# Cross-attention: softmax sums from a column of ones in the value tiles, output turned and normalised token by token

## Chip, cores and metric

The kernel runs on one NeuronCore of one Trainium2 chip, in one launch. The metric is device time in microseconds (us), from the start of the program to its end. Before the change it is 1276.02 us, the median of 3 runs (1275.25 to 1277.25).

## What is computed

One decoder layer over `x` of shape (16, 128, 256): a sparse self-attention, a cross-attention to a context of the same shape, and a mixture-of-experts feed-forward, each with a layer norm ahead of it and a residual behind it. Only the cross-attention bears on the change. Cut to what matters:

```python
x = x + self_attention(layernorm(x), ...)
x = x + xattn(layernorm(x), ctx, ctx)
x = x + experts(layernorm(x), ...)

def xattn(q, k, v):          # each (16, 128, 256); 8 heads
    qh = q.reshape(16 * 8, 16, 256)       # a head is 16 of the 128 rows
    kh = k.reshape(16 * 8, 16, 256)
    vh = v.reshape(16 * 8, 16, 256)
    qk = einsum('bdm,bdn->bmn', qh, kh) / sqrt(16)
    return einsum('bmn,bcn->bcm', softmax(qk, -1), vh).reshape(16, 128, 256)
```

So a head attends along the feature axis: 256 query columns m against 256 key columns n, and the 16 rows of the head are the contraction of the scores and the channels of the value.

## The kernel before, in words

Each engine runs its own program; they meet at semaphores only. The cross-attention stage is written by `cross_loads` (SP, the DMA queue), `cross_tensor` (PE), `cross_scalar` (ACT), `cross_vector` (DVE) and `cross_pool` (POOL). All five walk the same steps i = -4 to 17 (`STEPS`), as a software pipeline written out by hand, each step cut in four parts k = 0 to 3. In step i the stage works on several batches at once:

- `max_scores(i + 2)` on PE (line 1278): 8 times two matmuls of 112x256 into one of two banks (`XMAX`). `reduce_max` on DVE (line 1393) takes the row maxima of each bank; the next use of a bank waits for it.
- `shift_transposes(i + 1)` on PE (1289) turns the 8 maxima of a token, after all 8 reductions of that batch; ACT negates them (`keep_shift`, 1348) and SP writes them as a row of the query tile by DMA (1232).
- `score(i, k)` on PE (1264): two matmuls of 114x512 that give scores minus maxima into two of four banks; `softmax` on ACT (1341) writes the exponentials, 128x512 each, to `probs4`. `ctx_transposes` (1296) and `keep_values` (1356, 1357) make the value tile `xvalue`.
- `values(i - 1, piece)` on PE (1311), in pieces 0 to 7 of 4 matmuls, each 32 output rows wide, on fp32 data: pieces 0 to 3 multiply the probabilities by `xvalue` and pieces 4 to 7 by `ones_x`, so that the bank `XPV` holds the sums in its left half and each denominator, repeated for 16 rows, in its right half. In the trace each such matmul is two instructions, so a batch has 64. Pieces 0 to 2 follow in part k = 1, 3 to 5 in k = 2, 6 and 7 in k = 3.
- `normalised(i - 2)` on DVE: a reciprocal of 128x256 (1401), a multiplication (1403) into `xout`; it comes between reductions 0 and 1 of step i. `residual(i - 2)` on POOL (1448) adds `xout` to `X`, `next_stats` on DVE (210) takes the statistics for the next layer norm.
- `query_(i + 4)` on DVE (251) normalises the next queries, `query_high` on ACT (1364) makes their rounded part and `query_low` on POOL (1443) the rest; SP writes both to memory (1237, 1239) and reads them back head by head (1219), with the keys (1212), each queue entry in a fixed order.

PE executes in program order, so that whatever a matmul waits for holds up all that stands behind it. The order on PE in a step before is

```python
for k in range(4):
    score(i, k)
    if k == 0: shift_transposes(i + 1)
    if k == 2: ctx_transposes(i)
    max_scores(i + 2, 2 * k); max_scores(i + 2, 2 * k + 1)
    for piece in ((), (0, 1, 2), (3, 4, 5), (6, 7))[k]: values(i - 1, piece)
```

After the last batch the next stage (`moe_vector`, line 1725) waits until `X` is complete.

Of the kernel before, what the change touches and what calls it, by code (L numbers as in the profile page):

```python
# [7 lines left out]
ALU = mybir.AluOpType  # L8
ACT = mybir.ActivationFunctionType
# [3 lines left out]
B, T, D = 16, 128, 256  # L13
# [15 lines left out]
XH, XC = 8, 16  # L29
# [35 lines left out]
def build(nc, io):  # L65
    ctx = ExitStack()
    with ctx:
        place = [ctx]

        def sb(name, shape, dt=F32):  # L70
            return place[0].enter_context(nc.sbuf_tensor(name, shape, dt))
# [1107 lines left out]
        xvalue = [sb(f"xvalue{p}", [128, 2, XH, 32]) for p in range(2)]  # L1179
        ones_x = sb("ones_x", [128, 2, 32])  # L1180
        xmax = [sb(f"xmax{p}", [128, 2, XH]) for p in range(2)]
        xshift = [sb(f"xshift{p}", [XH, D], F32R) for p in range(2)]
        xden = sb("xden", [128, D])
        xout = [sb(f"xout{p}", [128, D]) for p in range(2)]
# [20 lines left out]
        def cross_loads(sp):  # L1205
# [19 lines left out]
            for b in range(B + 3):  # L1225
# [19 lines left out]
                if b < B:  # L1245
                    if b >= 2:
                        sp.wait_ge(S(f"ld_heads{p}"), 128 * (b // 2))
                    if b >= 4:
                        sp.wait_ge(S("xscore_done"), 4 * (b - 3))
                    load_keys(b, p, s)  # L1250
                    sp.wait_ge(S(f"xq_out{p}"), 32 * (b // 2 + 1))
                    load_queries(b, p, s)


        def cross_tensor(pe):
            def score(b, k):

                s = b % 4
                if k == 0:
                    pe.wait_ge(S(f"ld_shift{b % 2}"), 32 * (b // 2 + 1))  # L1260
                if 4 * b + k >= 2:
                    pe.wait_ge(S("xprob_ready"), 2 * (4 * b + k - 1))
                for c in range(2):
                    last = nc.tensor.matmul(XSCORE[2 * (k % 2) + c][:].rearrange("p (t m) -> p t m", t=2),  # L1264
                                            keys_x[s][0:XROWS + 2, k, c * 128:c * 128 + 128],
                                            query_x[s][0:XROWS + 2, k, :, :], start=True, stop=True)
                last.then_inc(S("xscore_done"), 1)

# [30 lines left out]

            def values(b, piece):  # L1300

                if piece == 0:
                    pe.wait_ge(S("xvalue_ready"), b + 1)
                    pe.wait_ge(S("xprob_ready"), 8 * b + 8)
                    if b:
                        pe.wait_ge(S("xpv_read"), b)
                den, hh, c = piece // 4, piece // 2 % 2, piece % 2
                for j in range(4):
                    h = 2 * j + hh
                    lhsT = ones_x[:, hh, :] if den else xvalue[b % 2][:, c, h, :]  # L1310
                    last = nc.tensor.matmul(XPV[32 * j:32 * j + 32, den * D:den * D + D], lhsT,  # L1311
                                            probs4[b % 2][:, 2 * (h % 4) + c, h // 4 * D:h // 4 * D + D],
                                            start=piece % 4 == 0, stop=piece % 4 == 3)
                if piece == 7:
                    last.then_inc(S("xpv_done"), 1)

            pe.wait_ge(S("cross_zeroed"), 2)
            pe.wait_ge(S("attn_added"), B)
            for i in STEPS:
                for k in range(4):  # L1320
                    if 0 <= i < B:
                        score(i, k)
                    if k == 0 and 0 <= i + 1 < B:
                        shift_transposes(i + 1)
                    if k == 2 and 0 <= i < B:
                        ctx_transposes(i)
                    if 0 <= i + 2 < B:
                        max_scores(i + 2, 2 * k)
                        max_scores(i + 2, 2 * k + 1)
                    if 0 <= i - 1 < B:  # L1330
                        for piece in ((), (0, 1, 2), (3, 4, 5), (6, 7))[k]:
                            values(i - 1, piece)


        def cross_scalar(act):
            def softmax(b, k):
                act.wait_ge(S("xscore_done"), 4 * b + k + 1)
                if k == 0 and b >= 2:
                    act.wait_ge(S("xpv_done"), b - 1)
                for c in range(2):  # L1340
                    nc.scalar.activation(probs4[b % 2][:, 2 * k + c, :], XSCORE[2 * (k % 2) + c][:], ACT.Exp,  # L1341
                                         scale=XSCALE).then_inc(S("xprob_ready"), 1)

# [6 lines left out]
            def keep_values(b):  # L1350
                act.wait_ge(S("ctxT_done"), b + 1)
                if b >= 2:
                    act.wait_ge(S("xpv_done"), b - 1)
                out = xvalue[b % 2][:].rearrange("p c (j two) x -> p (c j) (two x)", two=2)
                src = XT[:, 0:D].rearrange("p (j two x) -> p j two x", two=2, x=XC)
                nc.scalar.copy(out[:, :, 0:XC], src[:, :, 0, :])
                nc.scalar.copy(out[:, :, 48:64], src[:, :, 1, :]).then_inc(S("xvalue_ready"), 1)

# [11 lines left out]
            for i in STEPS:  # L1370
                for k in range(4):
                    if 0 <= i < B:
                        softmax(i, k)
                    if k == 0 and 0 <= i + 1 < B:
                        keep_shift(i + 1)
                    if k == 2 and 0 <= i < B:
                        keep_values(i)
                    if k == 1 and 0 <= i + 4 < B:
                        query_high(i + 4)


        def cross_vector(dve):
            def query_(b):
                if b >= 2:
                    dve.wait_ge(S("xq_lo_ready"), b - 1)
                normalise(xq[b % 2][:], b).then_inc(S("xq_ready"), 1)

            def reduce_max(b, m):
# [8 lines left out]
            def normalised(b):  # L1397
                dve.wait_ge(S("xpv_done"), b + 1)
                if b >= 2:
                    dve.wait_ge(S("xdone"), b - 1)  # L1400
# [9 lines left out]
            for p in range(2):  # L1410
                last = nc.vector.memset(xvalue[p][:], 0.0)
            nc.vector.memset(ones_x[:], 0.0).then_inc(S("vector_steps"), 1)
            dve.wait_ge(S("vector_steps"), 7)
            nc.vector.memset(ones_x[:, 0, 0:XC], 1.0)
            nc.vector.memset(ones_x[:, 1, XC:2 * XC], 1.0)
            for s in range(4):
# [5 lines left out]
            for i in STEPS:  # L1422
                for k in range(4):
                    if 0 <= i + 2 < B:
                        reduce_max(i + 2, 2 * k)
                    if k == 0 and 0 <= i - 2 < B:
                        normalised(i - 2)
                    if 0 <= i + 2 < B:
                        reduce_max(i + 2, 2 * k + 1)
                    if k == 1 and 0 <= i + 4 < B:  # L1430
                        query_(i + 4)
                    if k == 2 and 0 <= i - 2 < B:
                        next_stats(i - 2)


        def cross_pool(pool):
            def query_low(b):
                p = b % 2
# [6 lines left out]

            def residual(b):
                pool.wait_ge(S("xpv_read"), b + 1)
                nc.gpsimd.tensor_tensor(X[:, b, :], X[:, b, :], xout[b % 2][:], ALU.add).then_inc(S("xdone"), 1)
# [275 lines left out]
        def moe_vector(dve):  # L1724
            dve.wait_ge(S("xdone"), B)
            nc.vector.memset(zero_b[:], 0.0)
            nc.vector.memset(zero_b4[:], 0.0)
            nc.vector.memset(combine[:], 0.0).then_inc(S("moe_zeroed"), 1)
            ln_stats_vector(dve, 4)
# [303 lines left out]
```

## Time and profile before

| | |
|---|---|
| median of 3 runs | 1276.02 us |
| the profiled execution's own time | 1277.34 us |
| its span, first to last instruction | 1275.6 us |
| mean granted TensorE clock | 0.933 of full speed |
| busy: PE / DVE / ACT / POOL | 89% / 49% / 43% / 48% |
| self-attention and before | up to about 430 us |
| cross-attention | about 430 to 656 us |
| routing and experts | about 656 us to the end |

Busy shares are averages over stages with different limits. The rows further down are from the stage that is changed: a row of a window says how long each engine was busy in a stretch and what clock TensorE was granted (1.00 is 2.4 GHz, 0.50 is 1.2 GHz); a row of a timeline gives start, duration, engine, line, operation, tiles and count, and in brackets how long the engine stood idle before and what ended that.

### The profile page before, as it was taken

How to read it: one execution, taken by the hardware profiler on the slowest of the kernel's cores; microseconds unless marked ns; L12 is line 12 of the kernel's file. 1: busy time of each engine (PE TensorE's matmuls, PEld its weight loads, DVE VectorE, ACT ScalarE, POOL GpSimd, SP SyncE). 2: the span in 40 equal slices, each digit the busy share in tenths (PEclk: the TensorE clock that was granted, in tenths of full speed). 3: DMA queues.
4: the chain of work that ended last, by engine and by line, in shares of the span. 5: the costliest groups of instructions: out<-in, count | busy, mean ns of one | idle time of the engine just before them, and what ended most of it. 6: DMA issues, size and time to landing. Idle time of an engine off the chain costs nothing.

```text
span 1275.6 us, 23609 instructions
## 1 busy us (share of the span) xinstructions
PE 1137.3 (89%) x7920; PEld 911.9 (71%) x7920; DVE 628.4 (49%) x1343; ACT 553.9 (43%) x1185; POOL 612.5 (48%) x755
## 2 busy tenths in 40 slices
PE   5979999999999387878856899999999999999997
PEld 4757777777776254545444788888888788888886
DVE  5656777777777366566556233233233332323323
ACT  3326666666666334444443333333333233333331
POOL 3766565656563201110000566666666566666663
PEclk8969999999999668899885899999999999999998
DMA  5201010101010174344000544443344444334441
GB/s 121 59 1 30 25 31 22 28 25 31 23 29 23 35 164 97 90 103 100 19 1 22 128 108 115 115 110 102 105 114 116 119 115 115 104 104 109 115 115 54
DMA packets 74965, 96.99 MB, mean 76 GB/s; under 512 B 20412, under 2 KB 55868, under 8 KB 74892
## 3 DMA queue, kind: packets, MB, share of 16 engines
q1 hardware_dynamic: 74892, 96.05, 29.1%
q8 instruction: 42, 0.69, 0.2%
q14 instruction: 31, 0.25, 0.1%
HBM read 82.73 MB, written 13.12 MB: 75 GB/s over the span
## 4 chain that ended last, share of the span: by engine, by line
PE 56%; DVE 6%; issue 2%; ACT 1%; DMA 1%; POOL 0%; SPq 0%; POOLq 0%; DVEq 0%; ACTq 0%
PE bank L1589 28%; PE bank L1601 15%; PE bank L1311 5%; PE bank L1264 3%; PE bank L1278 2%; DVE xden L1401 2%; DVE xmax L1393 1%; DVE xout L1403 1%; DMA comb<-combine_scratch 0%; PE bank L1296 0%; PE bank L1289 0%; DVE X L1801 0%; DVE keys_x L1417 0%; PE bank L1564 0%; PE bank L1574 0%
## 5 line engine op out<-in xcount | busy, mean ns | idle before, releaser
L1815 POOL TENSOR_TENSOR hidden<-act_u,comb 128x512 f32<-128x512 f32 x132 | 217.5, 1648 | 214.9 <-DVE act_u L1783 144.0
L1783 DVE TENSOR_TENSOR act_u<-act_g,bank 128x512 f32<-128x512 f32 x132 | 90.8, 688 | 393.8 <-PE bank L1589 365.2
L1689 ACT ACTIVATE act_g<-bank 128x512 f32<-128x512 f32 x132 | 78.9, 598 | 356.5 <-PE bank L1589 356.5
L1589 PE MATMUL bank<-x_hi,up_hi 128*128 128x512 f32 x528 | 209.0, 396 | 5.8 <-POOL up_lo L1820 5.8
L1589 PE MATMUL bank<-x_lo,up_hi 128*128 128x512 f32 x528 | 208.2, 394 | 0.0
L1589 PE MATMUL bank<-x_hi,up_lo 128*128 128x512 f32 x528 | 206.5, 391 | 0.0
L1601 PE MATMUL bank<-down_hi,h_hi 128*128 128x256 f32 x528 | 149.4, 283 | 1.8 <-POOL down_lo L1825 1.8
L1601 PE MATMUL bank<-down_hi,h_lo 128*128 128x256 f32 x528 | 150.1, 284 | 0.0
L1601 PE MATMUL bank<-down_lo,h_hi 128*128 128x256 f32 x528 | 150.0, 284 | 0.0
L833 ACT ACTIVATE probs<-bank 128x512 f32<-128x512 f32 x192 | 113.8, 604 | 81.3 <-PE bank L656 44.5
L1393 DVE TENSOR_REDUCE xmax<-bank 128x2 f32<-128x512 f32 x128 | 83.5, 686 | 73.3 <-PE bank L1278 73.3
L1589 PEld LDWEIGHTS bank<-x_hi,up_hi 128*128 128x128 f32 x528 | 100.5, 190 | 25.0 <-POOL up_lo L1820 7.2
L1589 PEld LDWEIGHTS bank<-x_hi,up_lo 128*128 128x128 f32 x528 | 99.9, 189 | 21.9
L1341 ACT ACTIVATE probs<-bank 128x512 f32<-128x512 f32 x128 | 68.9, 590 | 107.4 <-PE bank L1264 107.4
L1589 PEld LDWEIGHTS bank<-x_lo,up_hi 128*128 128x128 f32 x528 | 100.5, 190 | 16.0
L1820 POOL TENSOR_TENSOR up_lo<-up_in,up_hi 128x512 fp32r<-128x512 f32 x66 | 85.0, 1287 | 48.1 <-ACT up_hi L1701 48.1
L1601 PEld LDWEIGHTS bank<-down_hi,h_hi 128*128 128x128 f32 x528 | 101.4, 192 | 7.1 <-POOL down_lo L1825 2.0
L1601 PEld LDWEIGHTS bank<-down_lo,h_hi 128*128 128x128 f32 x528 | 101.4, 192 | 5.0
L1601 PEld LDWEIGHTS bank<-down_hi,h_lo 128*128 128x128 f32 x528 | 101.5, 192 | 0.0
L1278 PE MATMUL bank<-keys_x,query_x 112*128 112x256 f32 x256 | 57.8, 346 | 48.0 <-DVE xmax L1393 28.1
L1787 DVE TENSOR_TENSOR h_lo<-hidden,h_hi 128x512 fp32r<-128x512 f32 x132 | 90.5, 686 | 1.8 <-ACT h_hi L1695 1.8
L952 DVE TENSOR_REDUCE blockmax<-bank 128x32 f32<-128x512 f32 x96 | 64.8, 690 | 51.9 <-PE bank L609 51.9
(258 smaller groups left out, 2246.3 us busy)
## 6 DMA issues: line engine op xcount, KB each, us to landing
comb<-combine_scratch SPq DMA_DIRECT2D x132, 256.0 KB, 3.9
up_in<-in_w_up SPq DMA_DIRECT2D x66, 256.0 KB, 3.5
down_in<-in_w_down SPq DMA_DIRECT2D x66, 128.0 KB, 3.8
keys_x<-key_rows_x SPq DMA_DIRECT2D x32, 192.0 KB, 3.3
key_rows_x<-ctx_hi SPq DMA_DIRECT2D x256, 16.0 KB, 1.5
query_x<-xq_rows_hi SPq DMA_DIRECT2D x64, 64.0 KB, 3.1
ctx_in<-in_ctx SPq DMA_DIRECT2D x16, 128.0 KB, 2.0
key_rows_x<-ctx_lo SPq DMA_DIRECT2D x128, 16.0 KB, 1.5
```

Of the source, the lines that this page charges most:

```text
L833: nc.scalar.activation(probs[:, u, :], SCORE[u % 2][:], ACT.Exp, scale=SCALE)\
L952: ins = nc.vector.tensor_reduce(blockmax[:, s, :, c0:c0 + 4], SMAX[m % 2][:].rearrange("p (h c k) -> p h c k", h=KV, k=BLK), AX, ALU.max)
L1278: last = nc.tensor.matmul(XMAX[m % 2][:, n * D:n * D + D], query_x[s][0:XROWS, k, pair // 2, c * 128:c * 128 + 128], keys_x[s][0:XROWS, k, ...
L1341: nc.scalar.activation(probs4[b % 2][:, 2 * k + c, :], XSCORE[2 * (k % 2) + c][:], ACT.Exp, scale=XSCALE).then_inc(S("xprob_ready"), 1)
L1393: nc.vector.tensor_reduce(xmax[b % 2][:, m // 4, hs:hs + 2], XMAX[m % 2][:].rearrange("p (h n) -> p h n", h=2), AX, ALU.max).then_inc(S(f" ...
L1589: last = nc.tensor.matmul(out[:], wp[p][:, c, s, :], xp[:, c, t:t + 512], start=k == 0, stop=k == 5)
L1601: last = nc.tensor.matmul(OUT[k // 2][:, k % 2 * D:k % 2 * D + D], hp[h][:, q * 128:q * 128 + 128], wp[p][:], start=False, stop=True, skip ...
L1689: nc.scalar.activation(act_g[h][:], GATE[h][:], ACT.Silu).then_inc(S(f"gated{h}"), 1)
L1783: nc.vector.tensor_tensor(act_u[h][:], act_g[h][:], UP[h][:], ALU.mult).then_inc(S(f"upped{h}"), 1)
L1787: nc.vector.tensor_tensor(h_lo[h][:], hidden[h][:], h_hi[h][:], ALU.subtract)\
L1815: nc.gpsimd.tensor_tensor(hidden[h][:], act_u[h][:], comb[p][:, 512 * h:512 * h + 512], ALU.mult)\
L1820: nc.gpsimd.tensor_tensor(up_lo[p][:], up_in[p][:], up_hi[p][:], ALU.subtract)\
```

## The change

The value tile gets a column of ones behind the 16 value columns of each head, so one matmul gives sums and denominator; `ones_x` and the four pieces that used it go. Both value groups (`hh` = 0 and 1, even and odd heads) are written to the two halves of the bank in one stretch. ACT copies that bank to `xpv`, PE transposes it in four 128x128 blocks into another bank (`XOUT`), DVE takes reciprocals of 128x16 and multiplies into `xnorm`, PE transposes that back in two blocks, and DVE adds it to `X`. Steps are cut in eight parts u instead of four, each with one score matmul pair half as large as before; the score banks are three instead of four. `query_` moves from DVE to POOL, the residual from POOL to DVE. `normalised` is a step earlier.

```diff
-        XSCORE = [bank[0], bank[1], bank[2], bank[3]]
-        XMAX = [bank[4], bank[5]]
-        XPV, XT = bank[6], bank[7]
+        XSCORE = [bank[0], bank[1], bank[2]]
+        XMAX = [bank[3], bank[4]]
+        XPV, XOUT, XT = bank[5], bank[6], bank[7]
...
+            def score(b, u):
+                s, k, c, n = b % 4, u // 2, u % 2, XH * b + u
...
+                if n >= 3:
+                    pe.wait_ge(S("xprob_ready"), n - 2)
+                nc.tensor.matmul(XSCORE[n % 3][:].rearrange("p (t m) -> p t m", t=2),
...
-            def values(b, piece):
+            def values(b, hh):
+                if hh == 0:
+                    pe.wait_ge(S("xvalue_ready"), b + 1)
+                    pe.wait_ge(S("xprob_ready"), 8 * b + 8)
+                    if b:
+                        pe.wait_ge(S("xpv_kept"), b)
+                for c in range(2):
+                    for j in range(4):
+                        h = 2 * j + hh
+                        last = nc.tensor.matmul(XPV[32 * j:32 * j + 32, hh * D:hh * D + D], xvalue[b % 2][:, c, h, :],
+                                                probs4[b % 2][:, 2 * (h % 4) + c, h // 4 * D:h // 4 * D + D],
+                                                start=c == 0, stop=c == 1)
...
+            def turn_values(b):
+                pe.wait_ge(S("xpv_kept"), b + 1)
+                if b:
+                    pe.wait_ge(S("xdone"), b)
+                for n in range(4):
+                    last = nc.tensor.transpose(XOUT[:, n * 128:n * 128 + 128], xpv[:, n * 128:n * 128 + 128], ident[:])
+                last.then_inc(S("xturned"), 1)
+
+            def turn_back(b):
+                pe.wait_ge(S("xnormed"), 2 * b + 2)
+                for n in range(2):
+                    last = nc.tensor.transpose(XOUT[:, n * 128:n * 128 + 128], xnorm[:, n * 128:n * 128 + 128], ident[:])
+                last.then_inc(S("xturned"), 1)
...
             for i in STEPS:
+                for u in range(XH):
                     if 0 <= i < B:
+                        score(i, u)
+                    if u == 0 and 0 <= i + 1 < B:
                         shift_transposes(i + 1)
+                    if 0 <= i + 2 < B:
+                        max_scores(i + 2, u)
+                    if u == 0 and 0 <= i - 2 < B:
+                        turn_back(i - 2)
+                    if u == 2 and 0 <= i - 1 < B:
+                        values(i - 1, 0)
+                        values(i - 1, 1)
+                    if u == 5 and 0 <= i - 1 < B:
+                        turn_values(i - 1)
+                    if u == 3 and 0 <= i < B:
                         ctx_transposes(i)
...
         def cross_scalar(act):
...
+                nc.scalar.copy(xvalue[b % 2][:, :, :, 0:XC], XT[:, 0:D].rearrange("p (c h x) -> p c h x", c=2, x=XC))\
+                    .then_inc(S("xvalue_ready"), 1)
+            def keep_pv(b):
+                act.wait_ge(S("xpv_done"), b + 1)
+                if b:
+                    act.wait_ge(S("xturned"), 2 * b - 1)
+                nc.scalar.copy(xpv[:], XPV[:]).then_inc(S("xpv_kept"), 1)
...
+                for u in range(XH):
                     if 0 <= i < B:
+                        softmax(i, u)
+                    if u == 0 and 0 <= i + 1 < B:
                         keep_shift(i + 1)
+                    if u == 2 and 0 <= i + 4 < B:
+                        query_high(i + 4)
+                    if u == 4 and 0 <= i - 1 < B:
+                        keep_pv(i - 1)
+                    if u == 5 and 0 <= i < B:
                         keep_values(i)
...
         def cross_vector(dve):
...
             def normalised(b):
-                nc.vector.reciprocal(xden[:], XPV[:, D:2 * D]).then_inc(S("xden_ready"), 1)
-                dve.wait_ge(S("xden_ready"), b + 1)
-                nc.vector.tensor_tensor(xout[b % 2][:], XPV[:, 0:D], xden[:], ALU.mult).then_inc(S("xpv_read"), 1)
+                dve.wait_ge(S("xturned"), 2 * b + 1)
+                src = XOUT[:].rearrange("p (hh mj x) -> p hh mj x", hh=2, x=32)
+                nc.vector.reciprocal(xden[:], src[:, :, :, XC]).then_inc(S("xnormed"), 1)
+                dve.wait_ge(S("xnormed"), 2 * b + 1)
+                nc.vector.tensor_tensor(xnorm[:]..., src[:, :, :, 0:XC], xden[:]..., ALU.mult).then_inc(S("xnormed"), 1)
+            def residual(b):
+                dve.wait_ge(S("xturned"), 2 * b + 2)
+                nc.vector.tensor_tensor(X[:, b, :], X[:, b, :], XOUT[:, 0:D], ALU.add).then_inc(S("xdone"), 1)
...
+                for u in range(XH):
                     if 0 <= i + 2 < B:
+                        reduce_max(i + 2, u)
+                    if u == 1 and 0 <= i - 2 < B:
+                        residual(i - 2)
+                    if u == 3 and 0 <= i - 2 < B:
                         next_stats(i - 2)
+                    if u == 6 and 0 <= i - 1 < B:
+                        normalised(i - 1)
...
         def cross_pool(pool):
+            def query_(b):
+                if b >= 2:
+                    pool.wait_ge(S("xq_lo_ready"), b - 1)
+                x = X[:, b, :]
+                nc.gpsimd.tensor_scalar(xq[b % 2][:], x, mean[:, b:b + 1], rstd[:, b:b + 1], ALU.subtract, ALU.mult)\
+                    .then_inc(S("xq_ready"), 1)
...
-            for i in STEPS:
-                if 0 <= i - 2 < B:
-                    residual(i - 2)
-                if 0 <= i + 4 < B:
-                    query_low(i + 4)
+            pool.wait_ge(S("xbias_ready"), 1)
+            for b in range(B):
+                query_(b)
+                query_low(b)
```

## Rows read from the trace of the kernel before

**Rows 1.** Windows: us; busy (instructions) PE, PEld, DVE, ACT, POOL; clock; DMA share; GB/s
```profile
320.00:420.00 100.00, 93.14 (x787) 71.80 (x785) 70.22 (x183) 64.56 (x136) 47.77 (x90) 1.00 0.10 25
447.84:460.98 13.14, 10.81 (x35) 8.11 (x36) 9.98 (x17) 0.86 (x2) 1.45 (x2) 0.50 0.78 165
468.45:478.23 9.78, 9.24 (x94) 5.45 (x92) 6.21 (x11) 5.50 (x13) 0.73 (x1) 1.00 0.62 149
480.07:493.16 13.09, 10.80 (x93) 6.19 (x92) 7.90 (x13) 5.27 (x14) 1.45 (x2) 0.87 0.39 90
519.24:530.72 11.48, 9.18 (x93) 5.61 (x92) 7.90 (x14) 5.27 (x14) 1.45 (x2) 1.00 0.45 106
618.88:630.18 11.30, 9.01 (x84) 5.38 (x84) 6.95 (x11) 3.71 (x10) 0.72 (x1) 0.85 0.05 14
638.10:646.01 7.91, 6.53 (x74) 3.32 (x74) 2.61 (x3) 4.56 (x11) 0.73 (x1) 1.00 0.00 0
```

**Rows 2.** Timeline of DVE: reciprocals of batch 0 and 11, then one step
```profile
480.07 1.75 DVE L1401 RECIPROCAL xden<-bank 128x256 f32<-128x256 f32 x1
...
618.88 1.75 DVE L1401 RECIPROCAL xden<-bank 128x256 f32<-128x256 f32 x1
...
568.26 1.75 DVE L1401 RECIPROCAL xden<-bank 128x256 f32<-128x256 f32 x1
570.04 0.42 DVE L1403 TENSOR_TENSOR xout<-bank,xden 128x256 f32<-128x256 f32 x1
570.39 1.97 DVE L1393 TENSOR_REDUCE xmax<-bank 128x2 f32<-128x512 f32 x3
```

**Rows 3.** Timeline of PE: one step at full clock
```profile
560.08 1.50 PE L1311 MATMUL bank<-probs,xvalue 128*32 128x256 f32 x24
561.51 0.73 PE L1264 MATMUL bank<-query_x,keys_x 114*128 114x512 f32 x2
562.08 0.38 PE L1296 MATMUL bank<-ident,ctx_v 128*128 128x128 f32 x2
562.21 0.72 PE L1278 MATMUL bank<-keys_x,query_x 112*128 112x256 f32 x4
562.86 0.64 PE L1311 MATMUL bank<-probs,xvalue 128*32 128x256 f32 x8
...
571.12 0.50 PE L1278 MATMUL bank<-keys_x,query_x 112*128 112x256 f32 x2 [2.22 <-DVE xmax L1393]
```

**Rows 4.** Timeline, end of the stage: PE's last values, POOL's residual, DVE's statistics
```profile
648.37 1.93 PE L1311 MATMUL bank<-probs,xvalue 128*32 128x256 f32 x32 [2.43 <-DVE xout L1403]
650.10 1.94 PE L1311 MATMUL bank<-probs,ones_x 128*32 128x256 f32 x32
...
655.14 0.43 DVE L210 BATCH_NORM_STATS2 stats<-X 128x6 f32<-128x256 f32 x1 [0.83 <-POOL X L1448]
```

**Rows 5.** Groups by line and shape: nearest rows for what is new
```profile
L1341 ACT ACTIVATE probs<-bank 128x512 f32<-128x512 f32 x128 | 68.9, 590 | 107.4 <-PE bank L1264 107.4
L840 ACT COPY pv<-bank 128x512 f32<-128x512 f32 x32 | 18.9, 592 | 1.1 <-PE bank L687 1.1
L973 DVE RECIPROCAL weight<-bank 128x32 f32<-128x32 f32 x32 | 11.0, 344 | 5.1 <-PE bank L698 5.1
L399 POOL TENSOR_SCALAR gates<-gates 128x96 f32<-128x96 f32 x16 | 9.8, 617 | 0.0
L251 DVE TENSOR_SCALAR xq<-X,mean,rstd 128x256 f32<-128x256 f32 x16 | 6.4, 406 | 0.0
```

**Rows 6.** Timeline of PE in the self-attention: four transposes and what follows
```profile
421.75 0.66 PE L698 MATMUL bank<-ident,pv 128*128 128x128 f32 x4
422.34 0.64 PE L687 MATMUL bank<-probs,value_near 128*32 128x256 f32 x8
```

**Rows 7.** Timeline of SP, the DMA queue
```profile
553.62 0.80 SPq L1212 DMA_DIRECT2D keys_x<-key_rows_x  x2
...
557.27 1.31 SPq L1232 DMA_DIRECT2D query_x<-xshift  x2
```

More of the change, by code:

```diff
@@ L1179, in build @@
         xvalue = [sb(f"xvalue{p}", [128, 2, XH, 32]) for p in range(2)]
-        ones_x = sb("ones_x", [128, 2, 32])
         xmax = [sb(f"xmax{p}", [128, 2, XH]) for p in range(2)]
         xshift = [sb(f"xshift{p}", [XH, D], F32R) for p in range(2)]
-        xden = sb("xden", [128, D])
-        xout = [sb(f"xout{p}", [128, D]) for p in range(2)]
+        xpv = sb("xpv", [128, 512])
+        xden = sb("xden", [128, 2, XH])
+        xnorm = sb("xnorm", [128, D])
         XROWS = 64 + 3 * XC
-        XSCORE = [bank[0], bank[1], bank[2], bank[3]]
-        XMAX = [bank[4], bank[5]]
-        XPV, XT = bank[6], bank[7]
+        XSCORE = [bank[0], bank[1], bank[2]]
+        XMAX = [bank[3], bank[4]]
+        XPV, XOUT, XT = bank[5], bank[6], bank[7]
         MAX_ORDER = (0, 2, 1, 3)
@@ L1255, in cross_tensor @@
         def cross_tensor(pe):
-            def score(b, k):
-                s = b % 4
-                if k == 0:
+            def score(b, u):
+                s, k, c, n = b % 4, u // 2, u % 2, XH * b + u
+                if u == 0:
                     pe.wait_ge(S(f"ld_shift{b % 2}"), 32 * (b // 2 + 1))
[L1261 to L1267, printed above, removed]
+                if n >= 3:
+                    pe.wait_ge(S("xprob_ready"), n - 2)
+                nc.tensor.matmul(XSCORE[n % 3][:].rearrange("p (t m) -> p t m", t=2),
+                                 keys_x[s][0:XROWS + 2, k, c * 128:c * 128 + 128],
+                                 query_x[s][0:XROWS + 2, k, :, :], start=True, stop=True)\
+                    .then_inc(S("xscore_done"), 1)
             def max_scores(b, m):
@@ L1305, in values @@
                     if b:
[L1306 to L1314, printed above, removed]
-                    last.then_inc(S("xpv_done"), 1)
+                        pe.wait_ge(S("xpv_kept"), b)
[5 more added lines that the diff above has]
+                                                start=c == 0, stop=c == 1)
+                if hh:
+                    last.then_inc(S("xpv_done"), 1)
+            def turn_values(b):
[10 more added lines that the diff above has]
+                last.then_inc(S("xturned"), 1)
             pe.wait_ge(S("cross_zeroed"), 2)
@@ L1319, in cross_tensor, with softmax @@
             for i in STEPS:
-                for k in range(4):
+                for u in range(XH):
                     if 0 <= i < B:
-                        score(i, k)
-                    if k == 0 and 0 <= i + 1 < B:
+                        score(i, u)
+                    if u == 0 and 0 <= i + 1 < B:
                         shift_transposes(i + 1)
-                    if k == 2 and 0 <= i < B:
-                        ctx_transposes(i)
[L1327 to L1332, printed above, removed]
+                    if 0 <= i + 2 < B:
[8 more added lines that the diff above has]
+                    if u == 3 and 0 <= i < B:
+                        ctx_transposes(i)
         def cross_scalar(act):
-            def softmax(b, k):
-                act.wait_ge(S("xscore_done"), 4 * b + k + 1)
-                if k == 0 and b >= 2:
+            def softmax(b, u):
+                n = XH * b + u
+                act.wait_ge(S("xscore_done"), n + 1)
+                if u == 0 and b >= 2:
                     act.wait_ge(S("xpv_done"), b - 1)
-                for c in range(2):
-                    nc.scalar.activation(probs4[b % 2][:, 2 * k + c, :], XSCORE[2 * (k % 2) + c][:], ACT.Exp,
-                                         scale=XSCALE).then_inc(S("xprob_ready"), 1)
+                nc.scalar.activation(probs4[b % 2][:, u, :], XSCORE[n % 3][:], ACT.Exp, scale=XSCALE)\
+                    .then_inc(S("xprob_ready"), 1)
             def keep_shift(b):
@@ L1411, in cross_vector @@
                 last = nc.vector.memset(xvalue[p][:], 0.0)
-            nc.vector.memset(ones_x[:], 0.0).then_inc(S("vector_steps"), 1)
+            last.then_inc(S("vector_steps"), 1)
             dve.wait_ge(S("vector_steps"), 7)
-            nc.vector.memset(ones_x[:, 0, 0:XC], 1.0)
-            nc.vector.memset(ones_x[:, 1, XC:2 * XC], 1.0)
+            for p in range(2):
+                nc.vector.memset(xvalue[p][:, :, :, XC:XC + 1], 1.0)
             for s in range(4):
@@ L1727, in moe_vector @@
             nc.vector.memset(zero_b4[:], 0.0)
-            nc.vector.memset(combine[:], 0.0).then_inc(S("moe_zeroed"), 1)
+            nc.vector.memset(combine[:], 0.0)
             ln_stats_vector(dve, 4)
```

35 lines of the change are left out of this document (4 added, 31 removed).

## The prediction

> **What bounds the kernel now.** I read the windows first: they say which engine fills the changed stage, and at what clock. The step before any reciprocal takes 9.78 us and PE is busy 9.24 of them (window 468.45) [rows 1]; later steps take 11.48 us at full clock and 13.09 at 0.87. PE holds the pace, but not by its work alone. The timeline of DVE gives the steady pace: reciprocals of batch 0 and batch 11 start at 480.07 and 618.88 us [rows 2], 138.81 us for 11 steps, 12.62 each. Then PE's timeline shows the hole: 2.22 us idle before a pair of `max_scores`, ended by a reduction [rows 3]. DVE shows why [rows 2]: behind reduction 0 stand the reciprocal (568.26 to 570.04) and its product, then reduction 1, whose bank PE wants back. And the hole has a second price: steps are of two kinds, 11.48 us at clock 1.00 and 13.0 to 13.1 at 0.87 [rows 1], 1.6 us dearer. Eight of the 11 are dear (3 x 11.48 + 8 x 13.05 = 138.8, which is the measured sum).
>
> **The terms of a new step**, all at full clock. On PE one score matmul takes 0.285 us of the stream (two from 561.51 to 562.08), a pair of `max_scores` as much (562.21 to 562.86 holds two pairs and a small lag), and a result is there some 0.2 us after the stream has moved on [rows 3].
> - Values: 64 instructions become 32. The stretch of 32 takes 650.10 - 648.37 = 1.73 us [rows 4]; cut in pieces it is 0.06 each (24 in 1.43 [rows 3]), 1.92. I take 1.85, against about 3.85 before: 2.0 us saved.
> - `turn_values`: four transposes, 422.34 - 421.75 = 0.59 us [rows 6]; 0.65 with its weights to load. `turn_back`: half of that, 0.3. No row has them in this stage; bounds are 0.13 a pair (562.08 to 562.21 [rows 3]) and twice the 0.59. So PE saves 1.1 us of its work.
> - ACT: one more copy of 128x512, 0.58 (0.592 [rows 5]); one value copy in place of two, nothing; eight exponentials of 0.59 [rows 5] as before, 4.7. With the queries (0.6), shift and value copies (0.8) about 6.7 us a step, hidden as long as a step is longer.
> - DVE: the reciprocal falls from 1.75 us [rows 2] to one of 128x16. Bounds: 0.344 (128x32 [rows 5]) and 0.11 (1.75 over 256 columns, times 16); I take 0.25. Product 0.42 as before, residual 0.42 (new on DVE), `query_` gone (0.41 [rows 5]). Total with eight reductions at 0.65: 5.2 + 0.25 + 0.42 + 0.42 + 0.42 = 6.7 us instead of about 7.9.
> - POOL: residual gone, `query_` comes. Bounds for 128x256: 0.41 (as fast as DVE) and 1.65 (617 ns for 96 columns, scaled) [rows 5]. It runs ahead of need and has the whole step; only the first delays anything: the first low part of the queries, by 0 to 1.2 us, once. I take 0.5. The Trainium skill, "GPSIMD Engine Reference", section 3.1, gives GpSimd some 2.6 cycles an element where VectorE has one for two-input work; by that, as an estimate, GpSimd would need two to three times DVE's time for this operation, which would cost a few tenths of a microsecond once. No run here shows it yet.
> - SP: the entries are the same. Keys to the shift rows are 557.27 - 553.62 = 3.65 us of issue, and the shift rows 1.31 [rows 7]; with three more entries some 6.3 us. Keys are wanted a whole step after their issue ends, so nothing here waits until a step is under about 8 us.
>
> **The walk through a step.** Zero is the end of the last reduction of the batch, for which `shift_transposes` waits. PE: shift pair to 0.25, max 0 to 0.54, `turn_back` to 0.8, score 1 and max 1 to 1.37, score 2 and max 2 to 1.94, values to 3.8, score 3 and max 3 to 4.37, context to 4.6, score 4 and max 4 to 5.2, score 5 and max 5 to 5.75. `turn_values` waits for ACT: score 4 is read from 5.0, exponential to 5.6, copy to 6.2. A wait of 0.5, then to 6.9; behind it stand score 6 and max 6, out at 7.7. DVE was free at 7.0 (reduction 5); reduction 6 to 8.4, reciprocal and product with their hops to 9.15, reduction 7 to 9.8. PE has meanwhile done score 7, max 7 and the next score 0 by 8.4, and stands idle 1.4 us. So what is late next is DVE's tail of two reductions with the normalisation between them, and the step is 9.8 us. Walking the step before in the same way gives its 11.48, since it is read from the same rows. Small hops are easily missed; I take 9.9.
>
> **The sum** against the profiled execution (1277.3 us; span 1275.6; the median of the runs is 1.3 lower).
> - 11 steps: 11 x (12.62 - 9.9) = 29.9, of which 11 x 1.16 = 12.8 is clock that I expect back.
> - The step of window 468.45 (9.78): nothing. The step of window 618.88, 11.30 to 9.9: 1.4.
> - Two steps without reductions, 7.9 each (window 638.10) [rows 1]: PE's stream 5.9 plus a wait of about 0.9 for ACT's copy, 6.8: 2.2 together.
> - End: before, PE came to the last values at 645.94 (648.37 less 2.43 of waiting), just as the last exponentials ended, and the last statistics end at 655.57 [rows 4]: 9.5 us from the exponentials. After: values 1.85 and hops 0.2, copy 0.7, turning 0.9, reciprocal and product 0.8, turning back 0.5, residual 0.5, statistics 0.5: 5.95. Saved 3.5.
> - Start: -0.5.
> Together 36.5. The experts' stage reads `X` later and is untouched. 1277.3 - 36.5 = 1240.8 for the profiled execution; 1240 for the median.
>
> **Rivals.**
> *The clock falls as before* (0.30). PE still has a hole of 1.4 us and a wait of 0.5 in every step. For: holes of 2.2 us brought half clock in 8 steps of 11. Against: the steps near the end have holes of over 1 us with PE busy 6.53 of 7.91 us at clock 1.00, and the self-attention runs 100 us at 1.00 with PE busy 93% [rows 1]. Price: the 12.8 us are not given back and a little more: 1254. The Trainium skill, "TensorE: Matmul & The Clock Gate", section "A second HAM failure mode: psum-queue depth-cycling", describes just such short idles between groups that make the clock swing. The steps of 13.09 us agree with it; those of 7.91 do not.
> *Slower: PE stays at half clock* (0.04). One mechanism: PE paced by DVE never gets back up. For: the window 447.84 shows PE busy 10.81 of 13.14 us at clock 0.50 throughout, paced by reductions. Price: about 7.7 us of stream becomes some 14, with the DVE tail 16 us a step; 13 x (16 - 12.5) = 45 more, 1322. It decides once PE's dense part no longer brings the clock up; after every hole before, it did, so little chance.
> *A longer ring PE, ACT, DVE* (0.08). `turn_values` has everything behind it. If values, copy, turning and normalisation run one after another with every hop longer, or the strided read of the bank costs DVE double, a step is near 11.5: 13 x 1.6 = 21 more, 1261.
> *The change does not do what it says*, PE's values not shrinking because the two groups in one stretch run slower (0.03): 2 us a step come back, partly under the waits: 1266; with the clock too, 1276, no change.
> *Better* (0.05): the hops hide, DVE's own 6.7 and PE's 7.7 us let a step be 9.0: 1228.
>
> **Numbers.** Forecast 0.50 at 1240, its own range 1230 to 1249. The range takes in the fallen clock with some longer steps: 1230 to 1259. Less than 0.2% (2.5 us) is about what a measurement of this kernel can tell from no change. Faster 0.93, same 0.02, slower 0.05.
>
> **What would show it.** Right: steps of 9.5 to 10.3 us; no reciprocal above 0.35 us; PE's longest idles 1.2 to 1.6 us, ended by a reduction before line 1289's transposes; 32 instructions of values a batch; clock 1.00 over the steady steps. The fallen clock would be seen as steps of two lengths again. The forecast is wrong if `turn_values` waits much over 0.5 us, if DVE's new reads of the turned bank are much over 0.42 us, or if PE waits for a DMA.

## The result, and the profile after

The changed kernel takes 1228.42 us (median of 4 runs, 1227.86 to 1228.62) against 1275.85 for the kernel before in the same comparison: a ratio of 0.9628, 95% interval 0.9612 to 0.9644. It is 47.4 us faster. The forecast was 1240 us with a range of 1230 to 1259: right in direction and in mechanism, short by 11.6 us in size. The result lies 1.6 us outside the range.

The windows of the two traces, cut at the same events, say where the time went. The rows below are of the kernel before, then of the kernel after; columns are start:end, us, busy us and instructions of PE, PEld, DVE, ACT and POOL, the granted clock, DMA share, GB/s. The cuts are: the last term of the layer norm, the first `max_scores`, the first score matmul of step 1, of step 2 and of step 14, the end of the last exponentials, the end of the last statistics.

```profile
439.71:447.84 8.13, 0.00 (x0) 0.03 (x1) 0.82 (x3) 1.69 (x3) 1.40 (x2) 0.50 0.58 161
447.84:468.45 20.61, 18.08 (x62) 13.43 (x63) 15.48 (x26) 6.08 (x14) 2.19 (x3) 0.55 0.77 165
478.23:630.04 151.81, 124.27 (x1108) 74.70 (x1104) 94.15 (x143) 62.25 (x142) 15.93 (x22) 0.90 0.36 86
630.04:646.06 16.02, 13.51 (x154) 7.01 (x150) 5.41 (x8) 9.34 (x21) 1.47 (x2) 1.00 0.01 2
646.06:655.57 9.51, 3.66 (x64) 2.39 (x64) 5.17 (x7) 1.29 (x2) 1.46 (x2) 1.00 0.01 2
655.57:1275.60 620.03, 586.09 (x3288) 513.89 (x3288) 204.28 (x403) 220.87 (x460) 345.50 (x264) 0.95 0.38 102
```

```profile
437.08:445.87 8.79, 0.00 (x0) 0.03 (x1) 0.17 (x1) 1.69 (x3) 7.01 (x7) 0.50 0.54 150
445.87:466.30 20.43, 17.57 (x62) 13.60 (x63) 14.78 (x23) 5.92 (x13) 3.87 (x4) 0.56 0.74 170
466.30:474.80 8.50, 7.49 (x66) 5.18 (x65) 5.13 (x9) 5.92 (x13) 1.93 (x2) 1.00 0.64 151
474.80:585.70 110.90, 90.86 (x795) 64.91 (x793) 76.82 (x145) 70.49 (x144) 18.16 (x19) 1.00 0.49 118
585.70:600.99 15.29, 11.43 (x102) 6.25 (x100) 4.73 (x13) 10.81 (x23) 0.00 (x0) 1.00 0.01 2
600.99:606.55 5.56, 3.03 (x38) 1.75 (x38) 2.32 (x7) 1.87 (x3) 0.00 (x0) 1.00 0.00 0
606.55:1226.10 619.55, 584.90 (x3286) 513.68 (x3288) 204.28 (x402) 220.77 (x460) 345.54 (x264) 0.95 0.38 102
```

Twelve full steps fell from 151.81 to 110.90 us: 40.9 of the 49.5 us between the two spans. Step 1, which is the 9.78 us of [rows 1], is 8.50. The end of the stage is 9.51 before and 5.56 after. The last exponentials of two steps without reductions gave only 0.7. The fill is the same and the start 0.7 longer. The remaining 3.1 us lie outside the change: 2.6 before the stage begins (439.71 against 437.08) and 0.5 behind it. The code ahead of the stage is the same in all kernels here, and the same point came at 437.1 to 440.8 us in the traces of this study, so those 2.6 us are, as far as these traces tell, a difference between executions and not a gain of the change.

One full step on DVE, PE and POOL after the change (timelines; start, duration, instruction, count, idle before; `...` marks rows left out):

```profile
521.34 0.25 DVE L1416 RECIPROCAL xden<-bank 128x16 f32<-128x16 f32 x1
521.62 0.42 DVE L1418 TENSOR_TENSOR xnorm<-bank,xden 128x256 f32<-128x256 f32 x1
521.96 0.68 DVE L1409 TENSOR_REDUCE xmax<-bank 128x2 f32<-128x512 f32 x1
...
529.97 0.69 DVE L1409 TENSOR_REDUCE xmax<-bank 128x2 f32<-128x512 f32 x1 [0.54 <-PE bank L1277]
530.58 0.25 DVE L1416 RECIPROCAL xden<-bank 128x16 f32<-128x16 f32 x1
530.86 0.42 DVE L1418 TENSOR_TENSOR xnorm<-bank,xden 128x256 f32<-128x256 f32 x1
531.20 0.68 DVE L1409 TENSOR_REDUCE xmax<-bank 128x2 f32<-128x512 f32 x1
```

```profile
522.75 0.38 PE L1288 MATMUL bank<-ident,xmax 128*8 128x128 f32 x2 [1.34 <-issue]
522.88 0.48 PE L1277 MATMUL bank<-keys_x,query_x 112*128 112x256 f32 x2
523.20 0.38 PE L1326 MATMUL bank<-ident,xnorm 128*128 128x128 f32 x2
...
524.57 1.93 PE L1309 MATMUL bank<-probs,xvalue 128*32 128x256 f32 x32
526.44 0.50 PE L1263 MATMUL bank<-query_x,keys_x 114*128 114x512 f32 x1
...
528.80 0.65 PE L1320 MATMUL bank<-ident,xpv 128*128 128x128 f32 x4 [0.33 <-ACT xpv L1376]
529.21 0.48 PE L1263 MATMUL bank<-query_x,keys_x 114*128 114x512 f32 x1
529.53 0.40 PE L1277 MATMUL bank<-keys_x,query_x 112*128 112x256 f32 x2
...
531.99 0.38 PE L1288 MATMUL bank<-ident,xmax 128*8 128x128 f32 x2 [1.34 <-issue]
```

The reader is to see three things. The reciprocal is 0.25 us where it was 1.75 [rows 2], and every step is 9.24 us (521.34 to 530.58). The hole on PE has moved, from a pair of `max_scores` [rows 3] to the transposes of the maxima (line 1288), and is 1.34 us instead of 2.22. The trace puts this idle down to "issue"; the row before on DVE tells what it is, since reduction 7 ends at 531.88 and the transposes start at 531.99. And one stretch of 32 value instructions takes 1.87 us (524.57 to 526.44), as costed.

### The profile page after: what moved, and what is told of

Read it like the earlier page. It is cut to its first block, busy times and chain, and to the rows that moved or that the text cites. A ratio compares the mean times of both kernels' runs of the same rounds, so it can differ in the third digit from the quotient of the medians.

```text
span 1226.1 us, 22759 instructions
## 1 busy us (share of the span) xinstructions
PE 1092.5 (89%) x7471; PEld 897.6 (73%) x7504; DVE 605.0 (49%) x1342; ACT 564.5 (46%) x1185; POOL 620.4 (51%) x755
## 4 chain that ended last, share of the span: by engine, by line
PE 55%; DVE 4%; issue 4%; ACT 2%; DMA 1%; POOL 0%; SPq 0%; POOLq 0%; DVEq 0%; ACTq 0%
PE bank L1609 29%; PE bank L1621 15%; PE bank L1309 2%; PE bank L1277 2%; PE bank L1263 2%; DVE xmax L1409 1%; PE bank L1320 1%; ACT xpv L1376 1%; PE bank L1288 1%; DMA comb<-combine_scratch 0%; PE bank L1326 0%; DVE X L1821 0%; DVE keys_x L1438 0%; PE bank L1584 0%; PE bank L1295 0%
## 5 line engine op out<-in xcount | busy, mean ns | idle before, releaser
L833 ACT ACTIVATE probs<-bank 128x512 f32<-128x512 f32 x192 | 113.8, 604 | 81.5 <-PE bank L656 44.7
L1840 POOL TENSOR_TENSOR up_lo<-up_in,up_hi 128x512 fp32r<-128x512 f32 x66 | 85.0, 1288 | 90.8 <-ACT up_hi L1721 90.8
L1356 ACT ACTIVATE probs<-bank 128x512 f32<-128x512 f32 x128 | 71.5, 600 | 39.3 <-PE bank L1263 37.8
L654 PE MATMUL bank<-query,keys 128*128 128x256 f32 x256 | 84.9, 356 | 0.5 <-ACT probs L833 0.4
```

What stands on the lines that cost most here:

```text
L654: nc.tensor.matmul(o, keys[p][:, kvh * 4 + j, :], query[p][:, kvh, 256:512], start=True, stop=False)
L833: nc.scalar.activation(probs[:, u, :], SCORE[u % 2][:], ACT.Exp, scale=SCALE)\
L1356: nc.scalar.activation(probs4[b % 2][:, u, :], XSCORE[n % 3][:], ACT.Exp, scale=XSCALE)\
L1840: nc.gpsimd.tensor_tensor(up_lo[p][:], up_in[p][:], up_hi[p][:], ALU.subtract)\
```

## The experiments

All medians are set against the kernel before in the same comparison; its medians there were 1275.4 to 1276.7 us. The diffs are cut to the lines that matter, with `...` for what is left out.

**1. The kernel before with a narrow reciprocal.** The product repeats 16 denominators, so the output is normalised with other values.

```diff
-                nc.vector.reciprocal(xden[:], XPV[:, D:2 * D]).then_inc(S("xden_ready"), 1)
+                nc.vector.reciprocal(xden[:, 0:16], XPV[:, D:D + 16]).then_inc(S("xden_ready"), 1)
...
```

> The kernel before, with its reciprocal over 16 of the 256 denominators only (the multiplication then repeats those 16, so the cross-attention's output is normalised with other values); nothing else is changed, PE still has its 64 value instructions a batch. Theory (the gain is mostly the hole that the wide reciprocal makes behind reduction 0, and the clock that the hole costs): a full step falls from 12.65 us on average to about 9.8, which is PE's own stream, at clock 1.00; with some 4 us at the end of the stage, about 1238 us. Rival (the gain is mostly PE's halved value work): the hole was only a symptom, a step stays above 11 us, about 1257 us or more.

Measured: 1238.71 us, ratio 0.9704 (0.9687 to 0.9720). The window over 11 steps, and PE's remaining hole:

```profile
479.10:588.88 109.78, 101.06 (x1013) 61.70 (x1012) 70.07 (x133) 57.49 (x133) 15.31 (x21) 1.00 0.50 114
```

```profile
520.38 0.50 PE L1278 MATMUL bank<-keys_x,query_x 112*128 112x256 f32 x2 [0.71 <-DVE xmax L1393]
```

9.98 us a step, at clock 1.00, with all 64 value instructions. So 38 of the 47 us are to be had by the width of the reciprocal alone: 1.5 us a step is the hole (2.22 to 0.71), and the remaining 1.14 are the clock, which is at 1.00 in all of these steps. The rival falls.

**2. The kernel after with its value matmuls issued twice.**

```diff
-                for c in range(2):
+                for c in (0, 1, 0, 1):
                     for j in range(4):
                         h = 2 * j + hh
```

> The kernel after, with each value matmul issued twice in its stretch (same results, 64 instructions a batch again). Theory (PE's stream up to the seventh pair of max_scores, and then DVE's tail, set the step, so that work in the stretch is on the path): each step is 1.87 us longer, 9.24 to 11.1, and the 16 batches add 30 us: about 1258 us. Rival (PE has slack in its idle times of 1.34 and 0.33 us a step): 0.2 to 0.5 us a step, about 1233 us.

Measured: 1258.01 us, ratio 0.9860 (0.9842 to 0.9879). Reciprocals come every 10.96 us, 1.72 more than in the kernel after, where 1.87 were expected; the stretch itself is 1.73 longer (3.66 against 1.93). Work in the stretch of values is on the path to the full; PE's two idle times do not absorb it, since they come later in the step and are as long as before:

```profile
523.42 0.38 PE L1288 MATMUL bank<-ident,xmax 128*8 128x128 f32 x2 [1.34 <-issue]
...
525.25 3.66 PE L1309 MATMUL bank<-probs,xvalue 128*32 128x256 f32 x64
```

**3. The kernel after with the normalisation behind the last reduction.**

```diff
-                    if u == 6 and 0 <= i - 1 < B:
+                    if u == 7 and 0 <= i - 1 < B:
                         normalised(i - 1)
```

> The kernel after, with the normalisation (reciprocal and product) on DVE behind reduction 7 of the step instead of behind reduction 6. Theory (PE waits at shift_transposes for DVE's tail: reduction 6, normalisation, reduction 7): 0.62 us leave the tail, PE's idle of 1.34 becomes 0.72, turn_back then waits some 0.1 to 0.2 us for the product; a step is 8.7 to 8.8 us, about 1222 us. Rival (the tail is not what ends last, or turn_back gives all of it back): 9.24 us a step, 1228 us.

Measured: 1221.37 us, ratio 0.9570 (0.9554 to 0.9586); a step is 8.67 us, and the hole is what it should be:

```profile
519.52 0.38 PE L1288 MATMUL bank<-ident,xmax 128*8 128x128 f32 x2 [0.72 <-DVE xmax L1409]
519.65 0.48 PE L1277 MATMUL bank<-keys_x,query_x 112*128 112x256 f32 x2
520.10 0.44 PE L1326 MATMUL bank<-ident,xnorm 128*128 128x128 f32 x2
```

0.62 us leave the hole, and the step gains 0.57 of them. `turn_back` now starts 0.45 us after the `max_scores` ahead of it (519.65 to 520.10) where it was 0.32. DVE's tail is what a step of the change ends with. This one line beats the change by 7 us.

**4. The kernel after with a reciprocal of 128x256 more**, its result unused.

```diff
...
+                nc.vector.reciprocal(xwide[:], XOUT[:, 0:D])
                 nc.vector.reciprocal(xden[:], src[:, :, :, XC]).then_inc(S("xnormed"), 1)
```

> The kernel after, with one more reciprocal of 128x256 on DVE (1.75 us, its result unused) ahead of the small one, so in the tail for which PE waits. Theory: a step is 1.75 us longer, PE's idle grows from 1.34 to 3.1 us, and with holes above those of the kernel before (2.2 us) the clock falls again in most steps, 1.6 us each time: 12.0 us on average, about 1265 us and clock below 1.00 in the steady steps. Rival (the clock does not hang on the hole but on the density of the rest): steps of 11.0 us at clock 1.00, about 1252 us.

Measured: 1286.70 us, ratio 1.0083 (1.0066 to 1.0101): the changed kernel with a reciprocal as wide as before is slower than the kernel before. The hole, and windows from one small reciprocal to the next:

```profile
519.29 0.59 PE L1289 MATMUL bank<-ident,xmax 128*8 128x128 f32 x2 [2.95 <-issue]
```

```profile
490.75:504.32 13.57, 10.29 (x66) 6.97 (x66) 8.01 (x14) 6.08 (x12) 1.93 (x2) 0.75 0.35 90
...
531.58:543.60 12.02, 8.73 (x66) 6.53 (x66) 8.02 (x14) 6.08 (x12) 1.94 (x2) 0.86 0.47 101
```

At full clock a step would be 10.9 us, an estimate from 9.24 and the longer hole. The steps are 12.0 to 13.6, 13.1 on average over twelve (475.58 to 632.76); the clock is 0.75 in eight of the twelve and 0.86 in four. So a longer hole, with the same stream on PE, brings the clock down. I had priced this at 1.1 us a step and it is 2.2.

**5. The same with half that width** (128x128), which makes the hole as long as in the kernel before.

```diff
...
+                nc.vector.reciprocal(xwide[:], XOUT[:, 0:128])
```

> The kernel after, with one more reciprocal of 128x128 on DVE (some 0.87 us, unused) ahead of the small one: PE's idle becomes about 2.2 us, as long as in the kernel before. Theory (the clock follows the hole): steps of 10.1 us at full clock, some of them 1.6 us longer at a granted clock below 1.00; if as often as before, 11.1 us on average, about 1252 us. Rival (a hole of 2.2 us is harmless in the new order, only 3 us are too much): 10.1 us each at clock 1.00, about 1240 us.

Measured: 1247.87 us (1242.95 to 1248.99), ratio 0.9783 (0.9768 to 0.9798), between the two expectations. The profiled execution is the fastest of them, 1242.95. Every step has a hole of 2.15 us; ten of the twelve are 10.05 us and two are longer, at a lower clock:

```profile
487.16:497.21 10.05, 7.57 (x67) 5.41 (x66) 7.21 (x14) 5.95 (x13) 1.94 (x2) 1.00 0.54 120
537.41:548.73 11.32, 8.84 (x67) 6.52 (x66) 7.21 (x14) 6.07 (x13) 1.94 (x2) 0.85 0.42 107
```

So a hole of this length brings the clock down sometimes. The other executions are 4.5 to 6 us slower and their mean granted clock is 0.937 to 0.942 against 0.944, so they probably had more such steps; they were not profiled.

**6. The kernel before with the narrow reciprocal and without the column sums**: half the value work, and no turning. The denominators are left out and 16 columns of the sums stand in for them.

```diff
-                        for piece in ((), (0, 1, 2), (3, 4, 5), (6, 7))[k]:
+                        for piece in ((), (0, 1, 2), (3,), ())[k]:
...
-                if piece == 7:
+                if piece == 3:
...
```

> The kernel before with the reciprocal of 128x16 and without the four value pieces on the column sums (32 value instructions a batch as in the change, but no turning: the denominators are left out and 16 columns of the sums stand in for them, so the output is not the attention's). Theory (a step of 9.98 us with the small reciprocal is PE's stream with a wait of 0.7 us): 1.9 us of stream less, but DVE's order then makes a hole, so a step is 8.1 to 8.6 us, about 1216 us; the turning of the change then costs 0.7 to 1.1 us a step. Rival (PE's stream is no longer what counts once the reciprocal is small): a step stays near 9.5 us, about 1232 us.

Measured: 1221.11 us, ratio 0.9589 (0.9559 to 0.9619). The full-clock steps are 8.81 us. PE is busy 1.9 us less (7.28 in the row below, 9.19 in a step of experiment 1) and the step lost only 1.17, because PE now waits at two places:

```profile
520.01 0.38 PE L1289 MATMUL bank<-ident,xmax 128*8 128x128 f32 x2 [0.72 <-DVE xmax L1393]
...
522.62 0.80 PE L1278 MATMUL bank<-keys_x,query_x 112*128 112x256 f32 x2 [0.71 <-DVE xmax L1393]
523.35 2.78 PE L1311 MATMUL bank<-probs,xvalue 128*32 128x256 f32 x24
```

```profile
512.48:521.27 8.79, 7.28 (x61) 4.55 (x60) 6.39 (x14) 5.40 (x12) 1.46 (x2) 1.00 0.58 137
521.27:531.65 10.38, 8.86 (x61) 5.08 (x60) 6.39 (x13) 5.40 (x12) 1.45 (x2) 0.84 0.46 116
```

The turned order of the change costs 9.24 - 8.81 = 0.43 us a step against this; I had expected 0.7 to 1.1. It is the price of that order and not of turning as such: experiment 3 turns as well and has steps of 8.67 us.

One full step of this kernel is 10.38 us at clock 0.84, and its rows are the ones above: right behind the second of two waits of 0.7 us the 24 value instructions take 2.78 us, where they took 1.50 before [rows 3]. The same comes once more behind the last full step: 2.79 us for these instructions at 577.71, and the window from 575.71 to 584.64 is at 0.81. No wait of PE in this stretch is longer than 0.74 us. So the clock can fall without one long hole; two short ones stood ahead of it both times. One of the three executions that were not profiled took 1228.88 us at a mean clock of 0.937, where the others have 0.945, and probably had more such steps.

**7. The kernel after with both value groups last in the step.** Copy, turning, normalisation and residual follow one step later. Only the added lines are shown; the old places of the same calls are removed.

```diff
+                    if u == 3 and 0 <= i - 2 < B:
+                        turn_values(i - 2)
+                    if u == 6 and 0 <= i - 2 < B:
+                        turn_back(i - 2)
+                    if u == 7 and 0 <= i - 1 < B:
+                        values(i - 1, 0)
+                        values(i - 1, 1)
...
+                    if u == 1 and 0 <= i - 2 < B:
+                        keep_pv(i - 2)
...
+                    if u == 4 and 0 <= i - 2 < B:
+                        normalised(i - 2)
+                    if u == 7 and 0 <= i - 2 < B:
+                        residual(i - 2)
+                        next_stats(i - 2)
```

> The kernel after in another order: both value groups stand last in their step on PE, between the last pair of max_scores and the wait for DVE's tail; copy, turning, normalisation, turning back and residual follow one step later (copy behind exponential 1, turning in part 3, normalisation behind reduction 4, turning back in part 6). Theory (PE idles 1.34 us for DVE's tail and 0.33 for ACT's copy, in a stream of 7.57 us): the values fill both holes, a step is 7.6 to 7.9 us at clock 1.00, about 1210 us. Rival (another engine's order takes over at once, DVE's 6.7 us or ACT's copies in front of an exponential): 8.5 us a step or more, 1219 us or above.

Measured: 1216.50 us, ratio 0.9537 (0.9513 to 0.9562), the fastest kernel of the study, 12 us below the change. The profiled execution is its slowest, 1219.69 us. A step is 8.28 us over the eleven steps of the window; PE is busy 88.03 of 91.07 us, so the hole is filled. But neither expectation was exact. While PE runs its 1.9 us of values DVE gets nothing (1.27 us idle), and afterwards it has four reductions to do without a break, so it is DVE that is behind; this is read from the rows and was not tried by itself.

```profile
483.18:574.25 91.07, 88.03 (x727) 59.28 (x726) 71.44 (x134) 61.58 (x131) 17.10 (x18) 1.00 0.56 134
```

```profile
520.95 2.58 DVE L1409 TENSOR_REDUCE xmax<-bank 128x2 f32<-128x512 f32 x4 [1.27 <-PE bank L1277]
523.97 0.69 DVE L1409 TENSOR_REDUCE xmax<-bank 128x2 f32<-128x512 f32 x1 [0.44 <-PE bank L1277]
```

**8. Experiment 7 with one value group in part 3, the other in part 7**, and with the residual and its statistics in part 1 of the step after. The diff is against experiment 7.

```diff
-                    if u == 7 and 0 <= i - 1 < B:
+                    if u == 3 and 0 <= i - 1 < B:
                         values(i - 1, 0)
+                    if u == 7 and 0 <= i - 1 < B:
                         values(i - 1, 1)
...
```

> As the order with both value groups last in the step, but one group (even heads) in part 3 and the other in part 7, and the residual with its statistics behind reduction 1 of the following step. Theory (the order before it was held at 8.28 us a step by DVE, which stood idle 1.27 us while PE ran 1.9 us of values in one piece, and was behind in the rest): with the values in two pieces of 0.93 us DVE is fed throughout, a step is 7.7 to 7.9 us, about 1210 us. Rival (one piece of 0.93 us does not cover DVE's tail, PE idles again): 8.3 us a step, about 1217 us.

Measured: 1223.53 us, ratio 0.9589 (0.9576 to 0.9602), a step of 8.67 us. The theory fell, and so did the rival, which had 8.3. DVE now has two long waits a step, 1.00 and 1.19 us, where experiment 7 has 1.27 and 0.44:

```profile
516.70 0.69 DVE L1410 TENSOR_REDUCE xmax<-bank 128x2 f32<-128x512 f32 x1 [1.00 <-PE bank L1277]
...
521.09 1.29 DVE L1410 TENSOR_REDUCE xmax<-bank 128x2 f32<-128x512 f32 x2 [1.19 <-PE bank L1277]
```

That is 0.48 us more of waiting, and the step is 0.39 longer. So with two banks between PE and DVE even 0.93 us without a new pair leaves DVE without work. One long stretch at the end of the step (8.28) did better than two short ones (8.67), and both better than the one in part 2 that the change has (9.24). The residual was moved too, and its part in this was not separated.

**What they give together, for a full step:** 12.62 us before; 9.98 with the narrow reciprocal (hole 1.5, clock 1.14); 8.81 with half the value work; 9.24 with the turning, which in this kernel is what makes a right output possible with a narrow reciprocal and half the value work.

## Why the prediction was short

| term | forecast, us | measured, us |
|---|---|---|
| 12 full steps | 31.3 | 40.9 |
| step 1 | 0 | 1.3 |
| two steps without reductions | 2.2 | 0.7 |
| end of the stage | 3.5 | 3.95 |
| start and fill | -0.5 | -0.5 |
| outside the stage | 0 | 3.1 |
| sum, profiled executions | 36.5 | 49.5 |

The medians moved by 47.4 us and not by 49.5, since the profiled execution before was 1.5 us above its median and the one after 0.6 below.

**The walk through a step** is the step of the prediction that failed, by its size: 9.9 us, measured 9.24, which is 7.9 us over twelve steps and more than the range was missed by. Its order was right. From the end of the last reduction (522.64 in the rows above) the values begin at 1.93 us (forecast 1.94) and the score behind them at 3.80 (3.8), `turn_values` waits for ACT's copy until 6.16 (6.2). Then three sizes were too large. The turning holds PE for 0.41 us (528.80 to 529.21), where I took 0.65: [rows 6] have 0.59 for four transposes, and I added 0.06 for weights. In [rows 6] values stand behind the transposes and here a score matmul does; the last section has the rows. Score 6 and max 6 are out at 7.3 (529.53 and 0.40), not 7.7. DVE's tail is 1.91 us (529.97 to 531.88), where I had 2.1: I added whole durations, 0.69 and 0.42, where in a stream one instruction starts 0.61 and 0.34 us after another, as the starts in [rows 2] already showed (570.04 to 570.39). Last, I put 0.1 us on top for hops that might be missed, with nothing in the rows for it.

**The step before** was taken between reciprocals, 138.81 us for 11 steps and 11.30 for the next. Between score matmuls, as the steps after are cut, the same twelve are 151.81 us. That is the other 1.7 us of this term: the reciprocal stands 1.84 us behind the first score matmul in step 2 and 0.14 in step 14, which has no reductions ahead of it.

**The clock** was forecast to come back in full, and did: 1.00 over all twelve steps, against 0.90. Its part in the eleven steps is 12.5 us (12.62 - 11.48 = 1.14 each), where I had written 12.8. The rival that it would fall as before had a mechanism that exists and a hole that was not enough for it here: with 1.34 us no step fell, with 2.15 us two of twelve did (experiment 5), with 2.95 us all twelve (experiment 4). The section of the Trainium skill that I cited for it, "A second HAM failure mode: psum-queue depth-cycling" of the page "TensorE: Matmul & The Clock Gate", names short idles between groups as the cause of a swinging clock. The runs agree that idles of 3 us and less can do it, and even two of 0.7 us (experiment 6); they also show 1.34 us in every step doing nothing. The rival by which PE stays at half clock did not come to pass: half clock ended in step 0, as before.

**Step 1** I had put at no gain. That was without a reason, since this step has the values of batch 0 too, and they are halved as well. PE's busy time in it falls from 9.24 to 7.49 us, its idle time grows from 0.54 to 1.01, and the step is 1.3 us shorter. It is also shorter than the steps behind it: no batch has a normalisation in DVE's tail yet, so PE idles 0.60 us at its start and not 1.34.

**The two steps without reductions** gave 0.7 of 2.2. The hole behind the very last reduction falls into the first of them (1.35 us at 587.45), and I had left it out. The wait for ACT's copy was as forecast, 0.96 us (0.9).

**The small terms.** The reciprocal of 128x16 is 0.250 us (forecast 0.25), ACT's copy 0.583 (0.58), `turn_back` 0.14 in the stream (0.3). `query_` on POOL is 1.22 us a piece, three times the 0.41 of DVE [rows 5]; the first low part came 0.7 us later (8.79 against 8.13 in the windows) and all others are hidden. The estimate from the Trainium skill, "GPSIMD Engine Reference", section 3.1, was two to three times DVE's time; this case's trace has 3.0 times. SP and the DMAs ended no wait on PE in a full step.

**The range.** Its lower end, 1230, rested on the walk. The better case at 1228 had a chance of 0.05 and was left outside. The result has its number but not its mechanism: a step is not 9.0 us, the hops are not hidden (PE still waits 1.34 and 0.33 us), and the rest came from step 1, from the step before and from outside the stage. In the walk every missed size pointed the same way, because each was rounded up on its own; the two steps without reductions pointed the other way. And of the 49.5 us, 2.6 lie in the part of the program ahead of the change, which no term had.

## What to carry to other kernels

When PE waits in program order for a bank that another engine empties, ask first what stands ahead of that engine's next release: here one wide reciprocal was worth 38 of 47 us, and the halved matmul work that comes with its removal about 1.2 us a step, of which the turned order took 0.43 back. Cost a hole of PE twice, once for its length and once for the clock, and look at the granted clock of every step even where the holes are short. When a step is walked through, use differences of starts from the rows, not durations, and do not round each hop up.

## What the runs showed of the hardware

The granted clock against the longest hole on PE, in the full steps of the profiled executions:

| kernel | longest hole, us | other waits in the step, us | clock |
|---|---|---|---|
| experiment 1 | 0.72 | none | 1.00 in 11 of 11 |
| experiment 6 | 0.74 | 0.72 | 0.84 in 1 of 11 |
| the change | 1.34 | 0.33 | 1.00 in 12 of 12 |
| experiment 5 | 2.15 | 0.33 | 0.85 in 2 of 12 |
| the kernel before | 2.22 | none | 0.87 in 8 of 11 |
| experiment 4 | 2.95 | 0.33 | 0.75 to 0.86 in 12 of 12 |

A lengthening of the hole by 1.61 us, from 1.34 to 2.95, cost 3.9 us a step. Neither the longest hole nor the sum of the waits puts these kernels in order: experiment 6 fell once with less of both than the change, and experiment 5 fell less often than the kernel before with more waiting. How often the clock falls also varies from one execution of a kernel to the next: those of the kernel before took 1269.8 us at a mean clock of 0.943 up to 1278.3 at 0.934. What exactly decides it is not settled by these runs.

Also not expected: four fp32 transposes hold PE for 0.41 us in the change, against 0.59 in [rows 6]. The wait ahead of them is not the reason. The kernel before has a case without a wait, with a matmul of 128x256 behind it, and in experiment 7 there is no wait either:

```profile
412.07 0.66 PE L698 MATMUL bank<-ident,pv 128*128 128x128 f32 x4
412.49 0.36 PE L662 MATMUL bank<-query,keys_near 128*128 128x256 f32 x1
```

```profile
522.63 0.60 PE L1320 MATMUL bank<-ident,xpv 128*128 128x128 f32 x4
523.07 0.38 PE L1295 MATMUL bank<-ident,ctx_v 128*128 128x128 f32 x2
```

That is 0.42 and 0.44 us. In experiment 8, where values 32 rows wide stand behind them, it is 0.56 (522.85 to 523.41). So the longer time goes with what follows, and the first of these rows stood in the trace of the kernel before. Why it does was not tried by itself.
